# A table of pairs for the two products of a blocked tridiagonalisation

## The reference

```python
deg = jnp.sum(A, axis=-1)                       # A: (64, 128, 128)
d_isqrt = jax.lax.rsqrt(deg)
Lap_norm = d_isqrt[..., :, None] * (deg[..., :, None] * eye - A) * d_isqrt[..., None, :]
_, U = jnp.linalg.eigh(Lap_norm)
agg = jnp.einsum('bmn,bmd->bnd', U, features)
h = relu(einsum('bnd,hd->bnh', agg, W0) + b0)
out = einsum('bnh,oh->bno', h, W1) + b1
ret = jnp.einsum('bnm,bmo->bno', U, out)
```

## Time and profile before

| | us |
|---|---|
| timed runs, median of 3 | 5151.7 (5149.34 to 5155.43) |
| profiled execution, whole | 5160.19 |
| its span | 5157.9 |
| DVE busy | 4163.5 (81% of the span) |
| PE busy | 2378.0 (46%) |
| ACT busy | 1313.2 (25%) |
| PE's mean granted clock | 0.686 |
| chain that ended last: DVE, PE, DMA | 60%, 27%, 5% |

### The profile page before, as it was taken

How to read it: one execution, slowest core, us unless ns; L and a number is a source line. 1 busy time by engine, 2 the same in 40 slices (tenths; PEclk the granted TensorE clock), 3 DMA queues, 4 the chain that set the end, 5 groups by cost and what they waited for, 6 DMA issues and landing times.

```text
span 5157.9 us, 57427 instructions
## 1 busy us (share of the span) xinstructions
PE 2378.0 (46%) x15702; PEld 1593.0 (31%) x15702; DVE 4163.5 (81%) x18604; ACT 1313.2 (25%) x4350; POOL 122.0 (2%) x53
## 2 busy tenths in 40 slices
PE   0555555555526717519349063344105821020399
PEld 0222222233324314215124063243105820020266
DVE  4788878888779999999999888686996979989522
ACT  0000000011113233242342233122442412224154
POOL 0000000000000000000000010010003100000000
PEclk9766666665556857758668576676557965555699
DMA  6000000000110000000000112005000030020120
GB/s 144 14 15 25 25 16 19 19 22 25 30 31 9 9 9 17 0 9 17 9 1 0 17 31 45 0 9 124 0 0 9 17 124 0 0 114 0 49 66 17
DMA packets 142060, 140.50 MB, mean 27 GB/s; under 512 B 28445, under 2 KB 128426, under 8 KB 134826
## 3 DMA queue, kind: packets, MB, share of 16 engines
q1 hardware_dynamic: 141738, 136.97, 9.8%
HBM read 110.43 MB, written 26.41 MB: 27 GB/s over the span
## 4 chain that ended last, share of the span: by engine, by line
DVE 60%; PE 27%; DMA 5%; issue 4%; ACT 3%; SPq 1%; DVEq 0%; ACTq 0%; PEldq 0%
PE psum L2038 7%; PE psum L1678 5%; DVE big_a L381 2%; DVE gvec L385 2%; DVE big_b L1107 2%; PE psum L2062 2%; DMA big_b<-rows_dram 1%; DVE vt L529 1%; PE psum L2240 1%; DVE big_b L716 1%; DMA vt<-pairs_dram 1%; DVE sc_t L951 1%; DVE big_b L707 1%; DVE big_b L711 1%; DVE big_a L953 1%
## 5 line engine op out<-in xcount | busy, mean ns | idle before, releaser
L2038 PE MATMUL psum<-big_a 128*32 128x508 f32 (+59 forms) x4032 | 443.7, 606 | 54.1 <-issue 50.9
L1627 PE MATMUL psum<-plane,big_a 128*128 128x128 f32 x192 | 50.2, 430 | 608.8 <-ACT big_a L1543 587.2
L2013 PE MATMUL psum<-plane,big_b 128*128 128x128 f32 x126 | 54.6, 433 | 442.7 <-DVE big_b L396 442.1
L2038 PEld LDWEIGHTS psum<-big_a 128*32 128x32 f32 x4032 | 174.3, 157 | 255.0 <-issue 175.5
L1678 PE MATMUL psum<-big_b 128*128 128x512 f32 x544 | 245.5, 613 | 0.0
L2234 PE MATMUL psum<-plane,big_b 128*128 128x128 f32 x192 | 37.7, 378 | 443.2 <-DVEq L1308 426.7
L2224 PE MATMUL psum<-big_b 128*128 128x128 f32 x384 | 71.7, 372 | 349.7 <-ACT big_b L2138 349.7
L1627 PEld LDWEIGHTS psum<-plane,big_a 128*128 128x128 f32 x192 | 36.0, 220 | 622.6 <-ACT big_a L1543 599.6
L1837 DVE TENSOR_REDUCE f_ln<-psum 128x4 f32<-128x512 f32 x32 | 22.1, 689 | 233.6 <-PE psum L1952 157.8
L1996 ACT COPY big_a<-psum 128x64 f32<-128x64 f32 x109 | 29.1, 267 | 662.7 <-PE psum L2047 662.7
L2219 PE MATMUL psum<-vt,big_b 128*128 128x128 f32 (+1 forms) x384 | 72.3, 375 | 261.1 <-ACT big_b L1330 261.1
(11 more groups left out here) (729 smaller groups left out, 9270.4 us busy)
## 6 DMA issues: line engine op xcount, KB each, us to landing
big_a<-rows_dram SPq DMA_DIRECT2D x4, 4096.0 KB, 13.9
vt<-pairs_dram SPq DMA_DIRECT2D x504, 32.0 KB
big_a<-rows_dram SPq DMA_DIRECT2D x4, 2048.0 KB, 17.3
pairs_dram<-big_a SPq DMA_DIRECT2D x252, 32.0 KB, 1.8
big_a<-rows_dram SPq DMA_DIRECT2D x2, 3072.0 KB, 15.6
big_b<-rows_dram SPq DMA_DIRECT2D x2, 3072.0 KB, 22.5
big_b<-adj SPq DMA_DIRECT2D x2, 2048.0 KB, 17.6
big_b<-adjT SPq DMA_DIRECT2D x2, 2048.0 KB, 39.5
```

Source lines behind the costliest of these rows:

```text
L1627: ins = t.transpose(psum[0:parts, bank, g * N:(g + 1) * N], src(g), ident)
L2013: t.transpose(psum[:, 1, 0:SLOTS], x_rows[0:SLOTS, k % 2, :], whole).then_inc(S("x_node_ps"), 1)
L2038: ins = t.matmul(psum[i * SPAN:i * SPAN + MW, 0, 0:4 * wide], v_masked[:, i, q * MW:(q + 1) * MW], anode[:, g:g + 4, k + 1:N + 2 * u], sta ...
```

## The change

The ring of vectors goes. In its place stands a table `past` (P) of 128 rows with 16 floats: row n holds entry n of v and w of all pairs of the panel, side by side. Both products now run row by row: they read 2u neighbours of P and write 2u neighbours of T, for each of the w rows; the 2u factors are read again for every row. L317 (now L318) takes its factors in place from row k + 1 of P, in swapped order. To fill the table, DVE copies w into a column of P at the start of the next `reflect` and v in `advance`, but in the last step of a panel, where no step follows that needs them. DVE writes v to one of 8 places `v_rows` in `big_b` and w to one of 4 places `w_rows`, and PE and SP read those.

```diff
         anode = carve(B, AW)
-        carve(AW)
-        ring = carve(PAIRS // 2, 2, N)
+        past = carve(N, PAIRS)
         terms = carve(N, 4 + PAIRS)
...
-        VR = PAIRS // 2
-        FULL = PANELS[2][0]
-        place = lambda k: k if k < FULL else (k - FULL) % VR
-        stored_before = lambda k: k - VR if k >= FULL + VR else k - FULL
-        x_rows = big_b[:, 0:2 * N].rearrange("p (k n) -> p k n", n=N)
+        VR = 8
+        v_rows = big_b[:, 0:VR * N].rearrange("p (k n) -> p k n", n=N)
+        x_rows = big_b[:, VR * N:(VR + 2) * N].rearrange("p (k n) -> p k n", n=N)
...
+            st(v.memset(w_rows[:, :, :], 0.0))
...
-            st(v.memset(ring[:, :, :, :], 0.0))
-            st(v.memset(big_b[:, 0:2 * N], 0.0))
+            st(v.memset(big_b[:, 0:(VR + 2) * N], 0.0))
...
                 n_x = lp.go(v.tensor_tensor_reduce(junk[:, x], raw[:, x], raw[:, x], 1.0, 0.0, ALU.mult, ALU.add, s2x))
-                if k >= FULL:
-                    v.wait_ge(S("v_stored"), 16 * (stored_before(k) + 1))
-                if k == FULL + VR - 2:
+                if j:
+                    v.wait_ge(S("w_row"), k)
+                    n_w = lp.go(v.tensor_copy(P[:, k + 1:, many - 1], w_rows[0:SLOTS, (k - 1) % 4, k + 1:]))
+                if k >= VR:
+                    v.wait_ge(S("v_stored"), 16 * (k - VR + 1))
+                if k == VR - 2:
                     v.wait_ge(S("lap_stored"), 48)
...
                 if j:
-                    pairs = pairs_of(k, u)
-                    partners = ring_h[:, place(k - u):place(k - u) + u, ::-1, k + 1]
-                    v.wait_ge(S("w_row"), k)
-                    lp.go(v.tensor_tensor(by_pair(T[:, live, 0:many]), pairs, over(partners, w, 3), ALU.mult))
-                    n_b = lp.n
+                    partners = P[:, k + 1, 0:many].rearrange("p (j t) -> p j t", t=2)[:, :, ::-1]
+                    lp.after(n_w)
+                    n_b = lp.go(v.tensor_tensor(by_pair(T[:, live, 0:many]), by_pair(P[:, live, 0:many]), over(partners, w, 1), ALU.mult))
...
-                    weights = coef[:, 0:many].rearrange("p (j t) -> p j t", t=2)
-                    lp.go(v.tensor_tensor(by_pair(T[:, live, 4:4 + many]), pairs_of(k, u), over(weights, w, 3), ALU.mult))
+                    lp.go(v.tensor_tensor(T[:, live, 4:4 + many], P[:, live, 0:many], over(coef[:, 0:many], w, 1), ALU.mult))
...
                 v.wait_ge(S("v_row"), k + 1)
+                if u < size - 1:
+                    lp.go(v.tensor_copy(P[:, k + 1:, many], vk))
...
-                if k >= FULL:
-                    v.wait_ge(S("w_stored"), 16 * (stored_before(k) + 1))
+                if k >= 4:
+                    v.wait_ge(S("w_stored"), (k - 3) * 16)
                 lp.after(n_s)
-                wn = ring_h[:, place(k), 1, live]
+                wn = w_rows[0:SLOTS, k % 4, live]
...
-            by_pair = lambda ap: ap.rearrange("p w (j t) -> p j t w", t=2)
-            pairs_of = lambda k, u: ring_h[:, place(k - u):place(k - u) + u, :, k + 1:]
+            by_pair = lambda ap: ap.rearrange("p w (j t) -> p w j t", t=2)
```

More of the change, by code:

```diff
@@ L142, in graph_net @@
         anode = carve(B, AW)
-        carve(AW)
-        ring = carve(PAIRS // 2, 2, N)
+        past = carve(N, PAIRS)
         terms = carve(N, 4 + PAIRS)
         PER = 16 // TILES
+        carve(AW)
         v_masked = carve(TILES, PER * (MW + 8))
@@ L283, in v_tridiagonal @@
             own = pl["own"][0:SLOTS, 0:4]
-            ring_h, T = ring[0:SLOTS], terms[0:SLOTS]
+            V = v_rows[0:SLOTS]
+            P, T = past[0:SLOTS], terms[0:SLOTS]
             d_, e_, tau_ = (tri_h[0:SLOTS, i, :] for i in range(3))
@@ L298, in reflect @@
                 be, tau = e_[:, k:k + 1], tau_[:, k:k + 1]
-                v_new = ring_h[:, place(k), 0, :]
+                v_new = V[:, k % VR, :]
                 v.wait_ge(S("x_row"), k + 1)
                 n_x = lp.go(v.tensor_tensor_reduce(junk[:, x], raw[:, x], raw[:, x], 1.0, 0.0, ALU.mult, ALU.add, s2x))
-                if k >= FULL:
-                    v.wait_ge(S("v_stored"), 16 * (stored_before(k) + 1))
-                if k == FULL + VR - 2:
+                if j:
[4 more added lines that the diff above has]
+                if k == VR - 2:
                     v.wait_ge(S("lap_stored"), 48)
@@ L353, in reflect, with advance @@
                 return n_e
-            def advance(k, u, n_e):
+            def advance(k, u, size, n_e):
                 j, w, many = u, N - k - 1, 2 * u
@@ L359, in advance @@
                 tau = tau_[:, k:k + 1]
-                vk = ring_h[:, place(k), 0, live]
+                vk = V[:, k % VR, live]
                 if not j:
@@ L422, in v_tridiagonal @@
                         n_e = reflect(b0 + u, u)
-                    advance(b0 + u, u, n_e)
+                    advance(b0 + u, u, size, n_e)
                     lp.rewind()
@@ L2024, in t_tridiagonal @@
                         t.wait_ge(S("w_row"), k)
-                        t.transpose(psum[:, 5, 0:SLOTS], ring[0:SLOTS, place(k - 1), 1, :], whole).then_inc(S("w_node_ps"), 1)
+                        t.transpose(psum[:, 5, 0:SLOTS], w_rows[0:SLOTS, (k - 1) % 4, :], whole).then_inc(S("w_node_ps"), 1)
                     t.wait_ge(S("x_weights"), k + 1)
@@ L2046, in t_tridiagonal @@
                         t.wait_ge(S("v_row"), k + 1)
-                        t.transpose(psum[:, 6, 0:SLOTS], ring[0:SLOTS, place(k), 0, :], whole).then_inc(S("v_node_ps"), 1)
+                        t.transpose(psum[:, 6, 0:SLOTS], v_rows[0:SLOTS, k % VR, :], whole).then_inc(S("v_node_ps"), 1)
                 b1 = b0 + size
@@ L2304, in _ @@
             sy.wait_ge(S("tri_started"), 2)
-            sy.dma_start(pairs_dram[N - 2:, 0].rearrange("k g n -> g k n"), ring[0::2, VR - 2:, 0, :]).then_inc(S("lap_stored"), 16)
+            sy.dma_start(pairs_dram[N - 2:, 0].rearrange("k g n -> g k n"), v_rows[0::2, VR - 2:, :]).then_inc(S("lap_stored"), 16)
             def pair_rows(k, u, c):
@@ L2316, in _ @@
                     sy.wait_ge(S("v_row"), k + 1)
-                    sy.dma_start(pairs_dram[k, 0], ring[0::2, place(k), 0, :]).then_inc(S("v_stored"), 16)
+                    sy.dma_start(pairs_dram[k, 0], v_rows[0::2, k % VR, :]).then_inc(S("v_stored"), 16)
                     if u:
@@ L2320, in _ @@
                     sy.wait_ge(S("w_row"), k + 1)
-                    sy.dma_start(pairs_dram[k, 1], ring[0::2, place(k), 1, :]).then_inc(S("w_stored"), 16)
+                    sy.dma_start(pairs_dram[k, 1], w_rows[0::2, k % 4, :]).then_inc(S("w_stored"), 16)
                     if u == 0 and k_panel:
```

## The result

The changed kernel takes 5081.6 us (median of 4, 5076.6 to 5097.7), the kernel before 5150.6 us on the same chip (here the median of 4 runs, one more than ahead of the prediction); the ratio of their times is 0.987, with a 95% interval of 0.985 to 0.989, that is 57 to 77 us less. Forecast were 35 us less and a time between 5098 and 5149 us, so the direction was right, and the size and the range were wrong.

The account below looks back on a forecast made before the run. The prediction took DVE to lead the changed stage (busy 1086 of 1353.5 us), PE late next. Its terms, -53 - 6 + 20 + 4 = -35 us, took the median from 5151.7 to 5117 us, range 5098 to 5149.

Parts of the forecast that it names:

- A: Second product, in advance behind the matvec: all its gain from neighbouring writes lies on the path, -53 us.
- B: First product, in reflect beside PE's matvec: only 6 of its 53 us gain shows, -6 us.
- C: Copy of w into the table in reflect: delays root request and matvec in 109 steps, +20 us, bounds 13 to 40.
- D: Copy of v in advance, between reduction and dot product, in 109 steps: +4 us, bounds 0 to +9.
- stretch: First to last start of the line giving x_row; the predicted sum of -35 us is set against it.
- The rule that each operation must wait until its predecessor's pipe has emptied: Both added copies on DVE would cost their whole duration, 29 and 13 us, making the sum -17 us.
- my theory of the stride: Both products: writes stepping 20 floats double the price; neighbours save 1.025 ns an element, 53 us of DVE time each.
- short runs: Rival on the products: runs of 2, 4 and 6 floats pay for each new row, 5128 us; chance within 0.70.
- The copies cost half and not twice: Rival on both added copies: each holds its engine 0.37 us, doubling +24 us, sum -11, 5141 us; chance 0.12.
- The slower case: Rival on both products: many short rows cause the doubled price, so 2.07 ns stays; +24 to +29 us, 5179; chance 0.10.
- The clock: Rival on PE's matvecs: shorter idle keeps the granted clock up, about 20 us more gain, 5097 us; chance 0.08.

Follow-up runs that it names:

- experiment 2: Changed kernel with its second product (in advance, behind the matvec) back to entries innermost; stretch 1315.2 us, median 5131.1 us, ratio to the kernel before 0.9972.
- experiment 1: Changed kernel with its first product (in reflect, beside the matvec) back to entries innermost; stretch 1272.7 us, median 5089.5 us, ratio to the kernel before 0.989.
- experiment 4: Changed kernel without the copy of w, table cleared once, so w's part is missing in both products; stretch 1268.4 us, median 5083.7 us.
- experiment 5: Kernel before with the wait for v_row moved to the small scaling, leaving the dot product one wait; stretch 1311.3 us, median 5135.8 against 5147.6 us.
- experiment 6: Changed kernel with the v_row wait at the small scaling and again at the dot product, giving it two waits; stretch 1276.5 us, one execution 5100.5 us.
- experiment 10: Changed kernel run again unaltered, against the kernel before; median 5085.8 against 5152.0 us, ratio 0.9868, stretch 1268.2 us.
- experiment 7: Changed kernel with one wait for each instruction of a step, two waits moved and one left out; stretch 1262.3 us, median 5079.7 us.
- experiment 8: Changed kernel with some 50 single products, copies and scalings of various strides added behind the last step to read prices; stretch 1269.1 or 1268.2 us unseparated, no median given.
- experiment 3: Changed kernel with a second copy of w into an unused table, right behind the first; stretch 1276.9 us, median 5096.1 us.

## Why the prediction failed

The steps, as it put them, against what the runs showed:

| step | predicted | measured |
|---|---|---|
| A, L381 behind the matvec | -53 | -48 (experiment 2): product -52.5, reduction behind it 0.04 us later a step |
| B, L317 beside the matvec | -6 | -3 to -5 (experiment 1) |
| C, copy of w | +20 | 0 on the stretch (experiment 4), at most +3 (the matvecs start 3.3 us later in sum) |
| D, copy of v | +4 | -9: copy about +5.5, second wait -14 (experiments 5, 6) |
| matvecs' own durations | 0 | +1.5, inside their scatter |
| panel ends | 0 | -4: about 1 is the same gap at the dot product in steps with u = 0, the rest open (317 to 322 us over all profiles) |
| stretch | -35 | -61 |
| medians less stretch | 0 | -6 to -8, cannot be told from 0 |

The mechanism was right: the doubled price came from the stride, the product behind the matvec gives nearly its whole gain, the one beside it nearly nothing, and PE is late next. Two terms were mis-sized, one of them in its sign.

*Term C* failed at "so the delay reaches PE too, and nothing hides it". The root request has to wait anyway: it needs the sum of squares, and starts 0.07 us behind the end of the accumulator's read (488.54 and 488.61 in the timeline after; on average 0.057 us, and 0.036 in the kernel before). The copy starts beside that read and lies in this wait. I had put L352's 272 ns and 0.187 us from start to start in its place, and added it behind the wait instead of inside it. My lower bound was 13 us, from short operations; zero had no reason against it, and by leaving it out I closed the range at the side on which the truth lay.

*Term D* failed at "L389 already waits for the reduction". It waited for two things, and the 0.15 us that I read as the latency of one was for the most part a second wait that stands in the queue as an instruction of its own. I had both pieces of order before me and read only that v_row's wait moves. With 0.04 us as the true latency, the copy costs 0.05 and the wait gives 0.13 a step (14.3 us over 109), of which 0.11 lie in the gap itself.

The measured terms add up to between -60 and -65 us; the stretch fell by 61. The two profiles alone split it without a margin. In the 109 steps the time from x_row to the matvec's start grew by 3.3 us, the matvecs by 1.5, the time from their end to L369 fell by 5.0 and from there to x_row by 56.8, and the other 16 steps with the panel ends fell by 3.9: -60.9. What is left of the medians' fall is not shown to exist: 61 us lie inside the interval of 57 to 77 us, and inside that of experiment 10, 60 to 76. Of the 26 us by which the forecast missed the stretch, C and D alone would make 30 to 33, and A gave 5 back.

The rule that each operation must wait until its predecessor's pipe has emptied, named as one against the change (the Trainium skill, page "VectorE: DVE Perf Modes", section "The DRAIN you can't avoid"), does not hold for copies here: they started every 0.12 us at 0.21 us each. The section itself adds that a next operation that is not held starts earlier, which the prediction left out and these starts bear out. The advice to save operations and not waits, which stands in that page's section "Rules for kernel authors", does not hold here either: experiments 5 and 7 saved waits alone, and their stretches fell by 16.9 and 5.0 us. The same skill's page "SBUF — State Buffer", section "Door 1: The DMA port swizzle (why `[64,N]` ≈ `[32,N]`)", says that memory is reached in lines of 16 bytes, four floats, and that an access in a new line pays unless each line is hit twice. The runs agree for writes: steps of 2 free, of 3 not quite, of 4 as dear as of 8 (1.06 and 1.08 us for 512 elements), runs of 2 free. They agree for reads in that these pay too, 1.67 ns, which my theory of the stride had left out; it changed nothing in the sum, since the products read neighbours before and after. The runs differ from the rule, read plainly, in one point: both steps meet a new line each time, yet a step of 16 cost a copy 0.05 us and one of 20 cost it 0.07.

The bounds of the prediction give 5151.7 - 53 = 5099 and 5151.7 - 4 = 5148; the range was put a microsecond wider at each end, which decides nothing. Its 1.045 ns an element stands in none of its rows (they give 1.06); experiment 8 gives 1.044.

The rivals: short runs pay nothing (experiment 8). The copies cost half and not twice (0.10 us for the second one in experiment 3). The slower case is gone, since no pattern of short rows paid. The clock gave nothing in the stage: the matvecs of the 109 steps sum to 376.9 us before and 378.4 after.

## What to carry to other kernels

Let the innermost loop of a vector operation write and read neighbours, even if a copy must keep a second layout for it: the copy goes where its engine waits for a result anyway. Before pricing an inserted instruction, look for the wait that it lands in, and count the waits of each instruction on the path: the second one had cost 0.11 us at every step and could be carried by a neighbour that waits for nothing. In both places where it cost something, the wait that ended last was the one split off in front; at the clearing of experiment 4, where both waits had already ended, a second one cost under 0.02 us. Where two engines run side by side, find which ends each half of a step before counting either's savings.

## What the runs showed that I had not expected

- A second wait on one DVE instruction is a record of its own in the queue and costs about 0.11 us at the dot product and 0.06 us at the write of w, even when what it waits for is long there.
- DVE starts a copy of 100 elements 0.12 us behind another though each lasts 0.21 us; and it starts one beside the accumulator's read.
- A factor held in SBUF adds 0.06 us to a scaling of 124 elements (0.285 against 0.225 us).
- Reads at steps of 16 floats cost 1.67 ns an element, writes at steps of 20 floats 2.09, both together no more than the write; neighbours cost 1.04.
